# Layer 2's features of a two-layer image network: centred convolution weights, chunks in pairs, and half-array matmuls

## The reference

```
def branch(xi):
    h = conv3x3(xi, conv1_w) + conv1_b            # 192 -> 64 channels, 'SAME'
    seq = h as (pixels, 64)
    xn = layer_norm(seq over the 64 channels) * norm1_w + norm1_b
    ym = mamba(xn, ...)                           # in_proj, causal conv of 4 taps, silu, scan, out_proj
    return ym + skip_scale * xn
v = group_norm(x)
y = concat([branch(v), branch(v flipped in width), branch(v flipped in height)])
y = layer_norm(y over 192) @ proj_w.T + proj_b
x = x + y
```

## Time and profile before

| | |
|---|---|
| median of 3 runs | 31563.71 us (31561.78 to 31573.28) |
| the profiled execution | 31560.8 us |
| its span, first to last instruction | 31559.0 us |
| mean granted TensorE clock | 0.966 |
| PE / DVE / ACT / POOL busy | 79% / 85% / 51% / 77% of the span |
| features stage of layer 2 | 22133 to 24957 us |
| output stage of layer 2 | 30620 us to the end |

### The profile page before, as it was taken

How to read it: one execution, slowest core, us unless ns; L and a number is a source line. 1 busy time by engine, 2 the same in 40 slices (tenths; PEclk the granted TensorE clock), 3 DMA queues, 4 the chain that set the end, 5 groups by cost and what they waited for, 6 DMA issues and landing times. The chain is left out here.

```text
span 31559.0 us, 218343 instructions
## 1 busy us (share of the span) xinstructions
PE 25016.3 (79%) x57532; PEld 9492.8 (30%) x57532; DVE 26869.6 (85%) x22560; ACT 16242.0 (51%) x26679; POOL 24325.1 (77%) x10344
## 2 busy tenths in 40 slices
PE   8777777777777777777777777766999888888877
PEld 3222222222222222222222222222333322222222
DVE  9899999999999999999999999964111399999984
ACT  2455555555555555555555555532222355555552
POOL 1799999999999999999999999951000266666652
PEclk9999999999999999999999999988999999999998
DMA  6433333333333333333333333355111244444456
GB/s 205 170 134 133 130 134 133 134 133 131 135 132 134 133 132 134 132 133 133 133 134 131 133 132 134 133 178 201 61 51 51 102 165 166 166 166 166 166 174 192
DMA packets 1142621, 4396.74 MB, mean 139 GB/s; under 512 B 247888, under 2 KB 285792, under 8 KB 776032
## 3 DMA queue, kind: packets, MB, share of 16 engines
q1 hardware_dynamic: 1035472, 4033.56, 34.6%
q10 hardware_dynamic: 105904, 349.22, 3.2%
HBM read 3715.33 MB, written 667.03 MB: 139 GB/s over the span
## 5 line engine op out<-in xcount | busy, mean ns | idle before, releaser
L856 DVE TENSOR_TENSOR_SCAN s_h<-s_dA,s_state,s_dbu 128x512 f32<-128x512 f32 x15296 | 18659.9, 1267 | 626.5 <-ACT s_dA L721 621.9
L794 POOL TENSOR_TENSOR s_dbu<-s_du,s_b_sb 128x1536 f32<-128x1536 f32 (+1 forms) x5634 | 17656.0, 3135 | 1467.0 <-DVE s_h L856 1441.0
L721 ACT ACTIVATE s_dA<-s_delta,s_negA 128x512 f32<-128x512 f32 x15360 | 10323.0, 685 | 6070.8 <-DVE s_h L856 6055.9
L596 PE MATMUL s_y_ps<-s_hc,s_ident 128*128 128x512 f32 x22528 | 10813.0, 602 | 0.6 <-DVE s_hc L866 0.5
L866 DVE TENSOR_TENSOR s_hc<-s_h,s_c_ps 128x1024 f32<-128x1024 f32 x5632 | 6737.1, 1196 | 238.1 <-issue 218.6
L586 PE MATMUL s_c_ps<-s_bc,s_sel 96*128 96x512 bf16 x7168 | 2553.9, 391 | 4952.7 <-DVE s_hc L866 4949.9
L596 PEld LDWEIGHTS s_y_ps<-s_hc,s_ident 128*128 128x128 f32 x22528 | 4386.9, 195 | 3497.7 <-issue 3190.9
L803 POOL TENSOR_TENSOR s_hc_pool<-s_h,s_c_sb 128x512 f32<-128x512 f32 x4096 | 5161.2, 1260 | 1.4 <-DVE s_h L856 1.3
L604 PE MATMUL s_y_ps<-s_hc_pool,s_ident 128*128 128x512 f32 x8192 | 4229.2, 598 | 0.0
L811 POOL TENSOR_TENSOR s_du<-s_delta,s_u 128x1536 f32<-128x1536 f32 (+1 forms) x450 | 1125.0, 2500 | 3350.4 <-ACT s_delta L708 3299.6
L586 PEld LDWEIGHTS s_c_ps<-s_bc,s_sel 96*128 96x128 bf16 x7168 | 575.1, 97 | 8696.9 <-DVE s_hc L866 8161.9
(11 more groups left out here) (131 smaller groups left out, 15106.4 us busy)
## 6 DMA issues: line engine op xcount, KB each, us to landing
s_b_sb<-rows SPq DMA_DIRECT2D x1794, 1024.0 KB, 4.7
s_c_sb<-rows SPq DMA_DIRECT2D x1024, 1024.0 KB, 6.2
s_u<-U SPq DMA_DIRECT2D x257, 768.0 KB
Y<-s_yo ACTq DMA_DIRECT2D x256, 768.0 KB, 3.3
m_y<-Y SPq DMA_DIRECT2D x192, 1024.0 KB, 7.5
s_u<-U SPq DMA_DIRECT2D x193, 256.0 KB
U<-f_row SPq DMA_DIRECT2D x24, 2048.0 KB, 17.3
U<-f_col SPq DMA_DIRECT2D x24, 2048.0 KB, 7.1
```

The source lines that it names most:

```text
L596: last = pe.matmul(y_ps[:, t, :], ident[:, :], hc[:, s % 2, j, :], start=False, stop=s == NS - 1 and j // nd == ng - 1)
L721: act.activation(dA[:, n % DECAYS, :], delta[g % 2][:, t, :], ACT.Exp, scale=negA[g % 2][:, a:a + 1]).then_inc(dA_ready, 1)
L794: pool.tensor_tensor(dbu[:, s % AHEAD, :, :], a, b, ALU.mult).then_inc(dbu_ready, 1)
L856: dve.tensor_tensor_scan(h[:, s % (2 * GROUP), j, :], dA[:, (n * J + j) % DECAYS, :], dbu[:, s % AHEAD, j, :], initial, ALU.mult, ALU.add) ...
```

## The change

- **Centred weights.** Once, at the stage's start, DVE subtracts from `w_pair` and `w_third` their mean over the 64 output channels of a branch, and from the bias its mean (PE computes that with `ones`). The convolution's result then has mean zero over the channels; `mean`, `centre` and `seq` go, and DVE's additions write `cen` directly.
- **Two chunks at a time.** Iteration i of four takes chunks i and 4 + i. Banks: FIRST (0, 1), SECOND (2, 3), THIRD (4), STAT (5 to 7). Variance, Ln, Exp, scale and squares work on three tiles of 512 columns: both chunks of branches 1 and 2, and one tile that holds the third branch of both chunks, the lower chunk in partitions 0 to 63 and the upper one in 64 to 127.
- **Third branch in column halves.** `conv_third` issues for each tap one matmul into PSUM partitions 0 to 63 and one into 64 to 127, both with 64 weight columns and each with its own chunk. `take_middle` copies its middle from the pair's bank with a second activation.
- **Projections in row halves.** Twelve jobs an image: eight of branches 1 and 2 (`xn_pair`, rows 0 to 63 and 64 to 127), four of the third branch's two halves (`xn_third`; a small DMA brings the 3 columns ahead of the second half). For each tap one matmul of each half, into two banks; then z the same way. The Silus take two banks at once. U and Z go out in 512 KB stores, a ring of four.
- **The end of an image.** Job 0, the last variance, the next image's group means, then jobs 1 to 11. Job 1 waits until Ln has read STAT and DVE has copied the group means. ACT finishes the layer norm before the first Silu.
- **Output stage.** XN's second slot is stored and loaded for 64 partitions only, in a DMA of its own; the rest is zeroed once.

```
-            def mean(b, c):
-                m = b * NCHUNK + c
-                pe.wait_ge(seq_ready, m + 1)
-                wait(pe, lnr_ready, m)
-                for slot in range(2):
-                    last = pe.matmul(stat_ps[:, slot, :], ones[:, :], seq[:, c % 2, slot, :], start=True, stop=True)
-                last.then_inc(mean_done, 1)
...
+            def conv_third(i):
+                upper, lower = rows_of(i)
+                for half in range(2):
+                    for k in OUTER:
+                        dy, dx = divmod(k, 3)
+                        for lo, c in ((0, lower), (CB, upper)):
+                            last = pe.matmul(ps[lo:lo + CB, THIRD, :], w_third[:, half, k, :],
+                                             pad[:, half, c * ROWS + dy:c * ROWS + dy + ROWS, dx:dx + W],
+                                             start=half == 0 and k == OUTER[0], stop=half == 1 and k == OUTER[-1])
+                last.then_inc(conv_done, 1)
...
+            def project(b, jb):
+                m = b * JOBS + jb
+                bank = jb % 2 * 4
+                if jb < NCHUNK:
+                    src, first = xn_pair, jb * T
+                    pe.wait_ge(xn_ready, b * PAIRS + min(jb + 1, PAIRS))
+                else:
+                    src, first = xn_third, (jb - NCHUNK) * T
+                    pe.wait_ge(halo_in, (b + 1) * 16)
+                if jb == 0:
+                    pe.wait_ge(taken, (b + 1) * PAIRS * 3 - 1)
+                    pe.wait_ge(middle_ready, (b + 1) * PAIRS * 4)
+                elif jb == 1:
+                    pe.wait_ge(lnr_ready, (b + 1) * PAIRS)
+                    pe.wait_ge(taken, (b + 1) * PAIRS * 3)
+                    if not is_last(b):
+                        pe.wait_ge(scale_steps, (b + 1) * SCALE_STEPS + 1)
+                else:
+                    pe.wait_ge(proj_read, 2 * (m - 2) + 1)
+                for k in range(DCONV):
+                    for lane in range(2):
+                        lo = lane * CB
+                        last = pe.matmul(ps[:, bank + lane, :], w_fold[lo:lo + CB, k, :],
+                                         src[lo:lo + CB, first + k:first + k + T],
+                                         start=k == 0, stop=k == DCONV - 1)
+                last.then_inc(proj_done, 1)
+                if jb > 1:
+                    pe.wait_ge(proj_read, 2 * (m - 2) + 2)
+                first += HALO
+                for lane in range(2):
+                    lo = lane * CB
+                    last = pe.matmul(ps[:, bank + 2 + lane, :], w_in[lo:lo + CB, D1:], src[lo:lo + CB, first:first + T],
+                                     start=True, stop=True)
+                last.then_inc(proj_done, 1)
...
+                for i in range(PAIRS):
+                    n = b * PAIRS + i
+                    upper, lower = rows_of(i)
+                    wait(pe, taken, (n - 1) * 3 + 1)
+                    conv(FIRST, upper, OUTER)
+                    wait(pe, middle_ready, (n - 1) * 4 + 2)
+                    conv(FIRST + 1, upper, MIDDLE)
+                    if i:
+                        variance(n - 1)
+                    wait(pe, taken, (n - 1) * 3 + 2)
+                    conv(SECOND, lower, OUTER)
+                    wait(pe, middle_ready, (n - 1) * 4 + 4)
+                    conv(SECOND + 1, lower, MIDDLE)
+                    wait(pe, taken, (n - 1) * 3 + 3)
+                    conv_third(i)
+
+                project(b, 0)
+                variance((b + 1) * PAIRS - 1)
                 if not is_last(b):
                     group_means(b + 1)
...
+                root((b + 1) * PAIRS - 1)
+                affine(b, PAIRS - 1)
                 if not is_last(b):
                     scale(b + 1)
-                for i in range(1, PARTS):
-                    take_proj(b, i)
+                for jb in range(JOBS):
+                    take_proj(b * JOBS + jb)
...
+            dve.tensor_reduce(w_mean[:, :, 0:2], pairs, mybir.AxisListType.X, ALU.add)
+            dve.tensor_reduce(w_mean[:, :, 2], third, mybir.AxisListType.X, ALU.add).then_inc(weights_ready, 1)
...
-                    sp.dma_start(xnb[:, c % 4, :, :], XN[b][:, :, c * T:(c + 1) * T]).then_inc(x_in[c % 4], 16)
+                    sp.dma_start(xnb[:, c % 4, 0, :], XN[b][:, 0, c * T:(c + 1) * T]).then_inc(x_in[c % 4], 16)
+                    sp.dma_start(xnb[0:CB, c % 4, 1, :], XN[b][0:CB, 1, c * T:(c + 1) * T]).then_inc(x_in[c % 4], 16)
```

More of the change, by code:

```diff
@@ L1245, in conv @@
                         dy, dx = divmod(k, 3)
-                        last = pe.matmul(bank_ps[0:rows, c % 2 * 3 + bank, :], w[:, half, k, :],
+                        last = pe.matmul(ps[:, bank, :], w_pair[:, half, k, :],
                                          pad[:, half, c * ROWS + dy:c * ROWS + dy + ROWS, dx:dx + W],
@@ L1267, in project @@
[L1267 to L1278, removed]
-                                         start=k == 0, stop=k == DCONV - 1)
[L1280 to L1284, removed]
+            def conv_third(i):
[8 more added lines that the diff above has]
+                last.then_inc(conv_done, 1)
@@ L1286, in image @@
             def image(b):
                 pe.wait_ge(pad_ready, b + 1)
[L1288 to L1298, removed]
-                pe.wait_ge(seq_ready, (b + 1) * NCHUNK)
@@ new lines, in affine @@
+            def affine(b, i):
+                n = b * PAIRS + i
+                act.wait_ge(scaled, n + 1)
+                if i == 0:
+                    wait(act, xn_stored, b * 48)
+                    wait(act, proj_done, b * JOBS * 2)
+                upper, lower = rows_of(i)
+                for slot, dst, at in ((0, xn_pair, upper), (1, xn_pair, lower), (2, xn_third, PAIRS - 1 - i)):
+                    first = HALO + at * T
+                    last = act.activation(dst[:, first:first + T], cen[:, n % 2, slot, :], ACT.Identity,
+                                          scale=ln_w[:, 0:1], bias=ln_b[:, 0:1])
+                last.then_inc(xn_ready, 1)
@@ L1418, in normalise @@
                 dve.wait_ge(setup, 5)
[L1420 removed]
+                wait(dve, conv_done, b * 5 * PAIRS)
                 for half in range(2):
@@ L1456, in image, with take_pair @@
-            def image(b):
-                for c in range(NCHUNK + 1):
-                    if c >= 1:
-                        centre(b, c - 1)
-                        scale(b, c - 1)
-                    if c < NCHUNK:
-                        take_conv(b, c)
-                    if c == 1 and not is_last(b):
+            def take_pair(n, second):
+                src = ps[:, SECOND if second else FIRST, :].rearrange("p (r w) -> p r w", w=W)
+                mid = middle[:, second, :].rearrange("p (r w) -> p r w", w=W)
+                dst = cen[:, n % 2, second, :].rearrange("p (r w) -> p r w", w=W)
+                dve.wait_ge(middle_ready, 4 * n + (3 if second else 1))
+                if not second:
+                    wait(dve, xn_ready, n - 1)
+                dve.tensor_tensor(dst[0:CB], src[0:CB], mid[0:CB], ALU.add)
+                dve.tensor_tensor(dst[CB:], src[CB:][:, :, ::-1], mid[CB:][:, :, ::-1], ALU.add).then_inc(taken, 1)
@@ L1464, in image @@
+            def image(b):
+                for i in range(PAIRS):
+                    n = b * PAIRS + i
+                    take_pair(n, 0)
+                    if i:
+                        scale(n - 1)
+                    take_pair(n, 1)
+                    take_third(n)
+                    if i == 1 and not is_last(b):
                         measure(b + 1)
+                scale((b + 1) * PAIRS - 1)
                 if not is_last(b):
```

249 lines of the change are left out of this document (117 added, 132 removed).

## The result

The changed kernel takes 30646.74 us (median of 4 runs, 30641.48 to 30654.45), the one before 31562.74: ratio 0.971, 95% interval 0.9693 to 0.9727. Forecast were 30630 and a range of 30590 to 30800.

A forecast was written before the change was run, and what follows sets the result against it. PE's passes were taken to bound layer 2's features stage; -924 there, +6 start, -3 tail and -13 output stage sum to -934 us, from 31560.8 to 30627, with 2.9 for the median 30630 us; range 30590 to 30800.

The forecast's parts named there:

- Count and price: PE in layer 2's features: 372 matmuls an image fit 264 slots of 0.858 us, 226.5 us, if halves overlap fully.
- The seam: Image end, from E, the last third convolution's end: job 1 at E+12.4, job 2 at E+18.5, PE idle 5.2 us.
- 924 saved, less 6, plus 3: Features of layer 2: 924 us saved in the images, 6 lost at the start on weights, 3 gained at the tail.
- The allowance of 8 us: Features stage: 8 us added to eight images' 1892 for accidental clock drops, giving 1900.
- The output stage: Layer 2's output: XN in two DMAs, fewer bytes against one more issue, -0.2 us 64 times, -13 us in all.
- The half clock that stays: Rival, chance 0.14: after the seam's wait the clock stays half through the projections, +176 us in all eight images, 30810.
- rows alone fail: Rival in the projections: row halves alone don't overlap, +412 us, 31040; chance 0.05 shared with columns alone failing.
- my 0.02 for slower: Chance 0.02 that the kernel gets slower: halves take turns and drain at each change, +240 us, 31800.
- The clock's own case: Rival, chance 0.14: half clock through the projections' remaining 47 us, priced 22 us an image, 30810, or 30720 if half do.
- the 1.8 already in the sum: Image seam: 1.8 us charged for a half clock of 3.6 us after PE's idle time.
- The weaker overlap in a long stream: Rival, chance 0.14: halves overlap less well over many passes, +104 us to twice that, 30730 to 30840.
- the queue worked out in the prediction: Features-stage stores: XN's 3 MB go ahead of U and Z; with four slots the needed store ends E+28.4, before E+30.5.

The follow-up runs named there:

- e1: The changed kernel with the third convolution's 12 matmuls of the lower chunk issued before all 12 of the upper, not in pairs; 30920.1 us.
- e10: The changed kernel with both matmuls of each projection pair on rows 0 to 63, so none can overlap; 31704.6 us, 1.004 of the kernel before.
- e3: The changed kernel with VectorE's copy of the group means and its small steps ahead of the image's last scale; 30655.6 us.
- e4: The changed kernel with VectorE's group-means copy before the last scale and ScalarE's first Silus right after the last Exp; 30616.0 us.
- e6: The kernel before the change with only the output stage's part of it, XN loaded in two DMAs; 31577.6 us, ratio 1.0002.
- e7: The changed kernel without the load of XN's second slot in the output stage, zeros standing in; 30585.7 us.
- e5: The changed kernel with two output slots instead of four (RING = 2); 30677.7 us.
- e2: The changed kernel with each projection job's four folded-tap matmuls of one half before the other half's four, z still paired; 30704.5 us.

## Why the prediction was right, step by step

- **Count and price.** 372 matmuls in 264 slots of 0.858 us: right. PE's records show the count, the 4.30 us a job and the 10.45 of a third convolution show the sharing. Both kinds of overlap are shown by taking them away: e1 for columns, e10 for rows. Of the 922.8 us saved in the images, by the count, 741 are the shared slots and 8 x 20 x 0.858 = 137 the matmuls that go; the other 44 are overhead, 134 us before and 89 after, part of it clock (0.97 in the stage before, 0.99 after). No run has the centred weights alone, so the two smaller parts are worked out and not shown. The price of a changed shape, 0.24 us, was what it was taken for.
- **The seam.** E+12.3 for E+12.4, 18.8 for 18.5, the stall at the variance 5.00 for 5.2. That a second wait, for the first Silu, stood just behind it is shown by e3. In the changed kernel it was only just hidden, because the half clock made job 1 longer: at full clock job 2 could have started at 22332.2, and that Silu ends at 22332.7. e4 takes it away, and leaves 1.6 us of the first.
- **The stage.** 924 saved, less 6, plus 3, is 921; measured 921.1, of which 922.8 saved in the images, 4.8 lost at the start and 3.0 saved at the tail. The allowance of 8 us was right in size (8 x 236.5 = 1892, measured 1901.5) and partly by luck. Some 5 us of it are spells of 6.8 us for 3.4, which make an image 1 to 1.5 us longer; but 3 are the first image's, whose first 5.7 us run at a clock of 0.50 from the stage's start, and which the sum did not have.
- **The output stage.** This is the term that was off: -13 forecast, +1.7 measured, 15 of the 17 us between forecast and result, though the stage spreads by about as much. I let the bytes win because more loads stood behind; e6 and e7 together say that the issue weighs as much as the bytes.
- **The rivals.** The half clock that stays did not come, and e10 shows why it was a fair rival: after the same wait it comes, and lasts 194.6 us, once the two halves don't overlap. So overlap and clock are not two cases but one. The case "rows alone fail" was put at 31040 as if the clock were a matter of its own; with it, it is 31705 (e10 stands in for it), on the other side of the kernel before. Its sign, and with it my 0.02 for slower, were too sure. The clock's own case was under-priced too. Half clock through the 47 us of work of jobs 1 to 11 costs an image those 47 us again, and not 22, which is the price of a spell that ends after 44; less the 1.8 already in the sum, eight images are +362 and 30990, outside the range that was to hold nearly all of this case. The weaker overlap in a long stream did not come: over 48 passes a shared slot takes 10.45 / 12 = 0.87 us, changes of shape included. The 78% that I had worked out from the Trainium skill, "TensorE: Matmul & The Clock Gate", Part 3 (Measured speedup), would have made it 1.10: it does not hold for two halves in a stream.
- **Stores.** Four slots leave one wait of 2.3 us in the stage, and two are too few (e5), as the queue worked out in the prediction says.

Left open: why the slow image spells before ended where they did. They lasted through the first part of the projections, which the last full-row variance follows; e10 speaks for the same cause, but no run moved that variance. Open, too, is why three of the eight waits of 5.60 us before led to such a long spell and the others, at the same place, to a short one.

## What to carry to other kernels

Look in the trace for a place where halves of the array already run side by side, however short: its records per microsecond are the proof, and the sum of slots follows. Halves must be issued as neighbours, or in blocks of a few passes in a long run of them (8 passes a row half cost 5%); two blocks of 24 column-half passes lose 20 of the 24 shared steps. Ask of every wait of PE both what stands behind it on the other engines and what passes come after it, since lone half-array passes can leave a clock that the wait halved at half until the work changes. And a load whose issue stands behind a wait for the loop's own end makes all loads behind it late: more slots there were worth 296 us, a third of what the rewriting of the features stage brought.

## What the runs showed of the hardware that was not expected

- Matmul passes to the other half of the array start ahead of up to four earlier passes of the first: 48 passes in two blocks of 24 took 19.16 us, which is 44 steps and not 48, with four doubled passes at the change (e1); blocks of 8 took 4.51 us a job for 4.29 in a run of jobs, with passes of a later matmul ahead of earlier ones, and 6.32 for 4.50 in a job by itself (e2).
- After a wait of 5.00 us, passes of 64 rows, one at a time and back to back, left the granted clock at 0.50 for 194.6 us, seven times out of seven; after a wait of 1.68 us the same passes ran at 1.00 for 95.2 us (e10). In pairs they had it back at 1.00 after 4.2 us of work in the image shown.
- Waits of 5.0 and of 3.8 us were followed by half clock, and a seam's wait of 1.6 us was not (e4, whose PE waits 1.4 to 2.0 us at several places of an image, 1.00 over 1879.5 us). The length of the wait alone does not decide: one of 1.36 us was followed by 3.4 us of half clock in e2, the same wait in the changed kernel was not.
